# Twelve places of 288 gathered rows: tiles of 128, 128 and 32 rows read by two transfers, in place of three tiles of 96 read by one

## What is computed

```python
x = x + tanh(g_xattn) * xattn(layernorm(x), ctx_512, ...)       # latent attention, 16 heads
# mixture of experts on x = layernorm(x), 1792 tokens
logits = x @ gate_w.T                                           # 64 experts
topv, topi = top_k(logits, 8);  rw = softmax(topv)
gu = einsum('nh,eih->nei', x, gu_w)                             # 512 -> 2 x 128 for each expert
inter = silu(gate) * up * W[:, :, None]
out = einsum('nei,ehi->nh', inter, dp_w)                        # 128 -> 512
out = out + sigmoid(x @ sh_gate1_w.T) * shared_expert(x)
x = x + tanh(g_ffn) * out
```

## Time and profile before

| | |
|---|---|
| median of three runs | 1497.38 us (1494.94, 1497.38, 1502.37) |
| profiled execution | 1504.56 us, span 1502.7 us |
| mean granted TensorE clock | 0.981 |
| TensorE matmul / weight load busy | 1411.7 us (94%) / 1156.9 us (77%) |
| VectorE / ScalarE / GpSimd busy | 1147.9 (76%) / 670.9 (45%) / 783.4 us (52%) |
| DMA | 380.11 MB, 253 GB/s over the span |
| places (expert stage) | about 1071 to 1412 us of the span |

### The profile page before, as it was taken

One profiled execution on the slowest core, in us unless ns is written; L12 is line 12 of the kernel. 1 busy time (PEld: TensorE's weight loads), 2 busy tenths in 40 slices (PEclk: granted clock), 3 DMA queues, 4 the chain that ended last, 5 costly groups with the idle time before them and its releaser, 6 DMA issues.

```text
span 1502.7 us, 25078 instructions
## 1 busy us (share of the span) xinstructions
PE 1411.7 (94%) x7680; PEld 1156.9 (77%) x7680; DVE 1147.9 (76%) x2603; ACT 670.9 (45%) x1558; POOL 783.4 (52%) x858
## 2 busy tenths in 40 slices
PE   7999999999999999999999999985499999999976
PEld 6767887877788787788787778763489998998743
DVE  6768883499886289989449988453488999998588
ACT  3332772011576011277201147230377778777521
POOL 4655772145675468877347887334235434333322
PEclk9999999999999999999999999997699999999999
DMA  8899896465797778730467861496899999999698
GB/s 265 297 324 313 276 297 203 129 196 186 225 297 222 250 227 256 226 97 11 139 217 231 255 225 42 139 351 206 277 330 314 338 359 360 364 334 338 209 427 366
DMA packets 164504, 380.11 MB, mean 253 GB/s; under 512 B 20088, under 2 KB 55570, under 8 KB 162578
## 3 DMA queue, kind: packets, MB, share of 16 engines
q1 hardware_dynamic: 110726, 245.49, 49.2%
q10 hardware_dynamic: 33036, 70.72, 14.3%
q0 software_dynamic: 20608, 62.28, 11.9%
HBM read 238.82 MB, written 139.59 MB: 252 GB/s over the span
## 4 chain that ended last, share of the span: by engine, by line
PE 69%; DVE 10%; DMA 8%; POOL 6%; issue 5%; ACT 2%; SPq 0%; ACTq 0%; POOLq 0%; DVEq 0%
PE bank L858 18%; PE bank L860 17%; PE bank L859 17%; PE bank L965 7%; DMA p_in<-parts 4%; PE bank L994 4%; DMA parts<-y_sb,to_row 3%; PE bank L1164 3%; POOL slot_rows L2039 2%; POOL q_rope L2022 2%; DVE q_sin L1322 1%; POOL prob L2028 1%; DVE row_max L1336 1%; PE bank L950 1%; PE bank L940 1%
## 5 line engine op out<-in xcount | busy, mean ns | idle before, releaser
L2022 POOL TENSOR_TENSOR q_rope<-q_rope,q_sin 128x448 f32<-128x448 f32 x192 | 215.3, 1151 | 121.0 <-DVE q_sin L1322 120.3
L2098 POOL DMA_INDIRECT parts<-y_sb,to_row x140 | 138.0, 986 | 216.1 <-ACT y_sb L1923 166.5
L2028 POOL TENSOR_TENSOR prob<-prob,row_inv 128x375 f32<-128x375 f32 x218 | 175.8, 813 | 80.1 <-DVE row_inv L1344 73.9
L2039 POOL DMA_INDIRECT slot_rows<-rows,pos_i x112 | 110.7, 988 | 105.8 <-DVE count L1430 76.2
L1322 DVE TENSOR_TENSOR q_sin<-bank,sin_q 128x448 f32<-128x448 f32 (+1 forms) x256 | 158.2, 618 | 4.0
L965 PE MATMUL bank<-q_rope,m_w 128*128 128x448 f32 x384 | 156.8, 542 | 2.2 <-POOL q_rope L2022 1.0
L1336 DVE TENSOR_REDUCE row_max<-bank 128x1 f32<-128x375 f32 x224 | 118.8, 535 | 36.2 <-PE bank L860 35.5
L1776 ACT ACTIVATE prob<-bank,row_max 128x375 f32<-128x375 f32 x224 | 128.3, 573 | 5.4 <-DVE row_max L1336 5.4
L1923 ACT ACTIVATE y_sb<-bank,own 96x512 f32<-96x512 f32 (+4 forms) x140 | 90.6, 686 | 72.2 <-PE bank L860 56.6
L1318 DVE TENSOR_TENSOR q_rope<-bank,cos_q 128x448 f32<-128x448 f32 x192 | 118.1, 615 | 0.2 <-POOL q_rope L2022 0.2
L994 PE MATMUL bank<-ident,prob 128*125 128x128 f32 x672 | 112.5, 276 | 3.0 <-DVE prob_t0l L1357 2.5
(11 more groups left out here) (374 smaller groups left out, 4386.6 us busy)
## 6 DMA issues: line engine op xcount, KB each, us to landing
w_ex<-in_w_ex SPq DMA_DIRECT2D x64, 768.0 KB
slot_rows<-blank SPq DMA_DIRECT2D x64, 612.0 KB
p_in<-parts SPq DMA_DIRECT2D x13, 2048.0 KB, 16.8
m_w<-m_dram SPq DMA_DIRECT2D x48, 192.0 KB, 3.5
x_g<-slot_rows ACTq DMA_DIRECT2D x16, 476.0 KB
x_g<-slot_rows ACTq DMA_DIRECT2D x12, 510.0 KB
wq_s0h<-wq_dram ACTq DMA_DIRECT2D x23, 256.0 KB
wq_s0l<-wq_dram ACTq DMA_DIRECT2D x23, 256.0 KB
```

What stands on the lines that cost most here:

```text
L2022: pool.tensor_tensor(o[:, c, :], o[:, c, :], q_sin[:, c, :], ALU.add).then_inc(s_radd, 1)
L2028: pool.tensor_tensor(prob[i][:], prob[i][:], row_inv[:, i:i + 1].to_broadcast([P, L]), ALU.mult)\
L2039: pool.indirect_dma_start(slot_rows, bass.IndirectOffsetOnAxis(ap=pos_i[i][:, k:k + 1], axis=0), rows[i][:], None).then_inc(s_slots[i], 16)
L2098: pool.indirect_dma_start(parts, bass.IndirectOffsetOnAxis(ap=to_row[x % NROW][0:size, t:t + 1], axis=0), y_sb[x % NY][t][0:size, :], None)\
```

## The change

The first kind of place becomes (128, 128, 32) with the same room of 288 rows and the same three tiles. Tile sizes are now a list for each place; the other kinds keep their shapes. A place's rows lie in `BLOCKS`: the first two tiles as one block of 128 partitions with two consecutive rows each (rows 0 to 255), the third as a second block of 32 partitions with one row each (rows 256 to 287). For the 12 places that gives two transfers instead of one, and each of the three instructions of `find_own` is issued twice, once for each block. Semaphore targets for the rows (`slots_read`) count 16 for each transfer.

```diff
-KINDS = ((12, 96, 3), (8, 128, 2), (12, 120, 2), (16, 112, 2), (8, 104, 2), (8, 96, 2))
+KINDS = ((12, (128, 128, 32)), (8, (128, 128)), (12, (120, 120)), (16, (112, 112)), (8, (104, 104)), (8, (96, 96)))
+TILES = [sizes for places, sizes in KINDS for _ in range(places)]
+BLOCKS = [[(0, sizes[0], 0, 2)] + [(2 * sizes[0], size, 2, 3) for size in sizes[2:]] for sizes in TILES]
...
+def slots_read(x):
+    return 16 * sum(len(BLOCKS[y]) for y in range(x % NXE, x + 1, NXE))
...
-            eng.dma_start(x_g[x % NXE][0:size, 0:n, :], slot_rows.rearrange("(e m) w -> e m w", m=SPAN)
-                         [bass.ds(e, 1), 0:size * n, :].rearrange("one (p t) w -> p (one t) w", t=n))\
-                .then_inc(s_xg[x % NXE], 16)
+            for start, size, t, end in BLOCKS[x]:
+                eng.dma_start(x_g[x % NXE][0:size, t:end, :], slot_rows.rearrange("(e m) w -> e m w", m=SPAN)
+                             [bass.ds(e, 1), start:start + size * (end - t), :]
+                             .rearrange("one (p t) w -> p (one t) w", t=end - t)).then_inc(s_xg[x % NXE], 16)
...
             def turn(x):
-                pe.wait_ge(s_xg[x % NXE], 16 * (x // NXE + 1))
-                for t in range(tiles):
+                pe.wait_ge(s_xg[x % NXE], slots_read(x))
+                for t, size in enumerate(TILES[x]):
...
             def find_own(x):
...
-                dve.scalar_tensor_tensor(found[0:size, 0:n, :], row[:, :, ID_AT:W_AT], order_f[0:size, x:x + 1],
-                                         row[:, :, W_AT:RW], ALU.is_equal, ALU.mult).then_inc(s_own, 1)
+                for _, size, t, end in BLOCKS[x]:
+                    row = x_g[x % NXE][0:size, t:end, :]
+                    m = dve.scalar_tensor_tensor(found[0:size, t:end, :], row[:, :, ID_AT:W_AT], order_f[0:size, x:x + 1],
+                                                 row[:, :, W_AT:RW], ALU.is_equal, ALU.mult)
+                m.then_inc(s_own, 1)
```

More of the change, by code:

```diff
@@ L40 @@
 TR = 96
-KINDS = ((12, 96, 3), (8, 128, 2), (12, 120, 2), (16, 112, 2), (8, 104, 2), (8, 96, 2))
-TILES = [(rows, n) for places, rows, n in KINDS for _ in range(places)]
-CAPS = [rows * n for rows, n in TILES]
-FIRST = [sum(n for _, n in TILES[:i]) for i in range(E + 1)]
+KINDS = ((12, (128, 128, 32)), (8, (128, 128)), (12, (120, 120)), (16, (112, 112)), (8, (104, 104)), (8, (96, 96)))
+TILES = [sizes for places, sizes in KINDS for _ in range(places)]
+CAPS = [sum(sizes) for sizes in TILES]
+FIRST = [sum(len(sizes) for sizes in TILES[:i]) for i in range(E + 1)]
+BLOCKS = [[(0, sizes[0], 0, 2)] + [(2 * sizes[0], size, 2, 3) for size in sizes[2:]] for sizes in TILES]
 CAP = max(CAPS)
@@ L50, with part_of @@
 SPARE = 1280
+def part_of(x, t):
+    start = sum(TILES[x][:t])
+    return slice(start, start + TILES[x][t])
+def slots_read(x):
+    return 16 * sum(len(BLOCKS[y]) for y in range(x % NXE, x + 1, NXE))
 def rope_tables(length, dim):
@@ L290, in rows_put @@
 def rows_put(x):
-    return sum(TILES[y][1] for y in range(x % NY, x + 1, NY))
+    return sum(len(TILES[y]) for y in range(x % NY, x + 1, NY))
 def build(nc, a, out):
@@ L1180, in down @@
             def down(x):
-                size, tiles = TILES[x]
                 pe.wait_ge(s_inner, 4 * (x + 1))
-                for t in range(tiles):
-                    if x and t < TILES[x - 1][1]:
+                for t, size in enumerate(TILES[x]):
+                    if x and t < len(TILES[x - 1]):
                         pe.wait_ge(s_y, FIRST[x - 1] + t + 1)
-                    products(bank[5 + t][0:size, :], [w[:, t * size:(t + 1) * size] for w in e_inner_s[x % 2]],
+                    products(bank[5 + t][0:size, :], [w[:, part_of(x, t)] for w in e_inner_s[x % 2]],
                              [w[:] for w in w_dp_s[x % 3]], True, True).then_inc(s_down, 1)
@@ L1556, in turn @@
             def turn(x):
-                size, tiles = TILES[x]
                 high, low = (t[:, 0:CJ * CAPS[x]].rearrange("p (j t) -> p j t", j=CJ) for t in xg_t[x % 2])
-                for t in range(tiles):
-                    n, part = FIRST[x] + t, slice(t * size, (t + 1) * size)
+                for t, size in enumerate(TILES[x]):
+                    n, part = FIRST[x] + t, part_of(x, t)
                     dve.wait_ge(s_et_a, n + 1)
@@ L1597, in find_own @@
                     dve.wait_ge(s_put[(x - NROW) % NY], 16 * rows_put(x - NROW))
[L1598 removed]
+                dve.wait_ge(s_xg[x % NXE], slots_read(x))
                 dve.wait_ge(s_own, 3 * x)
[L1600 to L1601 removed]
+                for _, size, t, end in BLOCKS[x]:
[3 more added lines that the diff above has]
+                m.then_inc(s_own, 1)
                 dve.wait_ge(s_own, 3 * x + 1)
[L1603 to L1605 removed]
+                for _, size, t, end in BLOCKS[x]:
+                    m = dve.tensor_reduce(own[x % NROW][0:size, t:end, :].rearrange("p t a -> p (t a)"),
+                                          found[0:size, t:end, :].rearrange("p t (a k) -> p (t a) k", a=2), AX_X, ALU.add)
+                m.then_inc(s_own, 1)
                 dve.wait_ge(s_own, 3 * x + 2)
                 first = x % NY * 3
[L1608 to L1609 removed]
+                for _, size, t, end in BLOCKS[x]:
+                    m = dve.tensor_tensor(to_row[x % NROW][0:size, t:end], own[x % NROW][0:size, t:end, 1],
+                                          spare[0:size, first + t:first + end], ALU.max)
+                m.then_inc(s_own, 1)
             split_expert(0)
@@ L1896, in turn @@
                         act.wait_ge(s_gu, x - 1)
-                    act.activation(high[:, :, t * size:(t + 1) * size],
+                    act.activation(high[:, :, part_of(x, t)],
                                    bank[n % 3][:, 0:CJ * size].rearrange("p (j t) -> p j t", j=CJ), ACT.Copy)\
```

4 lines of the change are left out of this document (removed).

## The result

The changed kernel took 1506.12 us (median of 20 runs, 1498.62 to 1514.07) where the kernel before took 1497.69 beside it (20 runs, 1493.18 to 1505.58): a ratio of 1.0043, interval 1.0027 to 1.0059. So it is slower, by about 2 to 6 us by the ratios, on the edge of what can be told from no change, and the 1498.5 forecast, range 1493 to 1504, was too low.

The account below looks back on a forecast made before the run. TensorE was taken to pace the 288-row places; +1.2 (TensorE) +0.3 (VectorE, once) + 0 (first read) - 0.4 (scatters) = +1.1 us on the median of 1497.38 gave 1498.5 us, range 1493 to 1504.

Parts of the forecast that it names:

- Rival 3: Expert stage, first places: DMA engines, not TensorE, set the pace; lighter load brings 6.29 to 5.9 us, 1491.8; chance 0.06.
- Rival 2: Row reads: packets cost 0.311 us whatever their size, DMA becomes the pace, 1508 to 1512, evictions wait for scatters; chance 0.06.
- two transfers to disjoint partitions: Row reads: the Trainium skill's rule that two such transfers bring nothing over one, cited as speaking against the split.
- the bound above of the four short transposes: 32-row tile on TensorE: each transpose at most today's 82.5 ns, four 0.33 us, place +0.21 us; 54 ns taken.
- the TensorE term of the sum: Transposes of the twelve 288-row places: 1.09 us for 0.99, +0.10 us each, +1.2 us in all, ends 0 and +2.5.
- the symptom that would prove it wrong: Transposes of the 32-row tile: prediction wrong if a small one costs far over 82 ns.
- The load rule: TensorE weight loads priced by columns, P / 1.2 ns: short transposes 107 ns each, +0.31 us a place, +3.7 us.
- rival 1: TensorE's small tile costs more, by the load rule or its upper end with VectorE's: 1501; chance 0.12.
- VectorE: `turn` unchanged at 1656 ns, small piece 284; `find_own` +0.3 us a place, covered; busy share to about 0.94.
- The one uncovered spot: Stage start, place 2: gate products wait for `e_half` behind `find_own`; 0.3 us once, ends 0 and 0.61.
- First read: Stage start, TensorE waiting 4.58 us for rows: change taken as 0, ends -0.27 and +0.54 us.
- less DMA: Places after 1195 us: cheaper reads give back TensorE time lost around scatters; -0.4 us, ends -0.94 and 0.

Follow-up runs that it names:

- repeat_small: Changed kernel with the four transposes of the 32-row tile issued twice in a row; pace 6.96 us a place, 1504.44 us (one run).
- the repeats: The changed kernel, unchanged, measured three more times beside the kernel before: 1501.49, 1503.55 and 1502.81 us, ratios 1.0012, 1.0026 and 1.0017.

## Why the prediction was wrong

**The bound was read rightly.** TensorE paced the places before and after (26.90 of 26.90 us busy), and the time came from what it issues. Rival 3 (DMA paces, faster) fell: no place became faster, and TensorE had no gap. The share went from 0.95 to 0.90, but that is the longer place, not a lighter load: 0.95 of 6.29 us and 0.90 of 6.71 us are both 6.0 us. Rival 2 (packets at a fixed price) fell too: 28.8% of 16 engines for 20 us is 92 engine-us for 547 packets, 0.17 each and 53 us a MB, where it was 0.311 and 55.5. Nor did an eviction wait for a scatter in the twelve places, in any of the four traces of the changed kernel, which was that rival's own sign. It was slower, but not by that mechanism. The two reads are also not the case of two transfers to disjoint partitions that the forecast held against them: the 32 rows go to partitions 0 to 31, which the first transfer fills too.

**The step that failed is the bound above of the four short transposes.** The forecast took "no less than now for each, 82.5 ns, four to 0.33 us, the place +0.21 us" as its upper end and 54 ns as its value. The short transpose itself was near the value: 62 ns, four to 0.25, where 0.22 was said. What was missing is a term of its own, the border between tall and short weight loads, 0.26 us twelve times: the TensorE term of the sum, +1.2 us, measured +3.1 to +4.3 over the stage. The border was left out because every cost was taken as a price for each instruction, so the upper end, where a 32-column transpose costs what a 96-column one does, looked like a bound; it bounds the instruction, not its neighbourhood. And the trace of the kernel before did hold it, in a stretch that the forecast never looked at, because only the expert stage changes. In attention's part `fold_m` (L940) loads w_m on 64 partitions between loads of 128, 96 loads in 16 groups of six:

```profile
16.18 0.19 PEld L860 LDWEIGHTS bank<-xn_th,wq_s0l 128*128 128x128 f32 x1
16.68 0.74 PEld L940 LDWEIGHTS bank<-w_m 64*128 64x128 f32 x6 [0.31 <-issue]
17.54 0.19 PEld L858 LDWEIGHTS bank<-xn_th,wq_s1h 128*128 128x128 f32 x1
...
20.18 0.74 PEld L940 LDWEIGHTS bank<-w_m 64*128 64x128 f32 x6 [0.31 <-issue]
```

The loading stops for 0.31 us ahead of each group (5.0 us over all 16), released by nothing. This stop, taken as the price of the border once for each place, would have given 12 x 0.31 = 3.7 us on top of the 1.2 (an estimate: in the changed kernel the stop is 0.17 and the border costs 0.26). The forecast looked for the nearest row by the number of moving columns; the row to look for was the one with the same kind of step. The text even named the symptom that would prove it wrong, a small transpose "far over 82 ns": read as a price for each it is (0.42 + 0.12) / 4 = 135 ns, 0.12 being what the tall eight save against twelve of 96 columns.

**The load rule.** The forecast set against it that transposes follow each other every 82.5 ns. It is also wrong from the other side: a load of 32 partitions by 128 columns is recorded with 136 ns, as long as one of 128 by 128 with 141, which agrees with what the Trainium skill (TensorE: Matmul & The Clock Gate, LDWEIGHTS) says of equal columns, but the loads overlap and follow each other every 62 ns (`repeat_small`) where the rule has 107. Its sum of +3.7 us came near the stage's +3.8, and rival 1's 1501 near the repeats, by luck: the load that the rule makes dear is not what costs.

**From pace to stage.** Twelve times 0.42 would be 5.0 us. The eight settled places show 53.68 - 50.34 = 3.34, in each trace. The first four show 0.98, 0.46, -0.20 and 0.44 instead of 1.68, where TensorE still waits for others; that a longer turn falls partly into those waits is the likely reason, not a shown one, and each figure is against the one trace of the kernel before. The stage is +4.3, +3.8, +3.1 and +3.8 us longer. The sum had simply multiplied by twelve.

**VectorE.** As said: 281 ns for the small piece (284 predicted), 685 for the large ones, no product waiting for `e_half` after the start. Its busy share is 0.84, not 0.94, since the place itself grew. The one uncovered spot went from a wait of 0.24 us to 0.45, +0.21 where 0.3 was said:

```profile
1093.30 0.37 PE L868 MATMUL bank<-xg_t0h,w_gu_s0h 128*128 128x288 f32 x1 [0.45 <-DVE e_half L1585]
```

**First read and scatters.** From its issue at 1069.24 to the first transpose at 1073.53 the start took 4.29 us, before 4.63 (1066.42 to 1071.05): -0.34 where 0 was taken and -0.27 was the lower end. Evictions waited for scatters for 19.3 us in 15 waits, before 15.6 in 11; the other three traces of the changed kernel have 11.1 in 8, 13.9 in 11 and 18.2 in 14, so this figure scatters by more than it moved. The -0.4 of "less DMA" did not come: TensorE lost 1.02 us in 1202 to 1307 where it lost 0.94 in the same places before (1195 to 1300). In what lies behind the twelve places nothing can be told: 354.9 to 357.2 us over the four traces of the changed kernel, 357.0 before.

**From the stage to the total.** With the stage at +3.8 and the rest at nothing the forecast would have been 1497.4 + 3.8, about 1501, inside the range, and three of the four measurements (1501.49, 1503.55, 1502.81) lie there. The first one, 1506.12, is another 3 to 5 us up. There 11 of 20 runs have the mark of the gap at the end of attention, and the nine without it have a median of 1500.73: so the longer stage explains about 4 us of this result, and the share of runs with the gap most of the rest. That second part is read from the runs' clocks, which are not on record for the kernel before in this set; it was not tested. The range failed on that side too. The forecast had three runs to take the scatter from, 2.4 us below their median to 5.0 above, and a working of -1.2 to +3.7. Added up, these give 1493.8 to 1506.1; the range stopped at 1504 without saying why.

## What to carry to other kernels

A tile's cost is not only its own instructions: when a shape is new to an engine, price the step between it and its neighbours, and do not close the range above by the price of the nearest single instruction. On TensorE keep the contraction height of successive matmuls above 64 rows (32 and 64 paid next to tall ones, 80 to 128 did not; whether 32 next to 64 pays was not run): three equal tiles of 96 beat two full ones and a rest of 32, and where a rest is unavoidable, let it be 80 rows or more, pad it (32 up to 96 gained 0.20 us a place here), or put all short ones together so that the border is crossed once. And take the pace of a repeated step from the trace as the measure, since it resolves 0.01 us where the totals of this kernel resolve several. Where totals fall into two groups, look for the mark that parts them before comparing medians.

## What the hardware showed that I had not expected

- Going from loads of 128 partitions to loads of 32 and back costs TensorE about 0.26 us at a granted clock of 1.00 (from 112 to 64 and back about 0.32, an estimate), visible as a stop of 0.17 us (0.14) in the loads that nothing releases and as a longer first product behind (0.33 for 0.16 us). Ahead of the loads of 64 partitions in attention the stop is 0.31 us. Neither weights narrow in columns (128 partitions by 32 columns) nor few moving columns over 128 partitions (64 of them) cost anything of the kind.
- Transposes of 32 columns follow each other every 62 ns when their neighbours are alike.
- Two executions of the same kernel can differ by 8 us in when attention ends (1073.53 and 1065.66 for the first transposes behind it), where TensorE stands for most of 10 us or not at all, and the granted clock falls with it (0.75 against 1.00 in the window from 1020).
